# A layer norm's row chain and its scaling step cut into two column halves, in a macaron transformer layer on 8 cores

## The chip, the cores and the metric

The kernel runs on all 8 cores of one Trainium2 chip. The metric is the device time in microseconds of the slowest core, for one execution. A profile adds, for each core, the span from its first to its last instruction and the mean clock that was granted to TensorE.

## What is computed

One macaron layer over 2 x 4096 rows of width 2048: half a feed-forward block, an attention block, half a feed-forward block, each behind a layer norm.

```python
def _layernorm(x, axis=-1, eps=1e-5):
    m = jnp.mean(x, axis=axis, keepdims=True)
    v = jnp.var(x, axis=axis, keepdims=True)
    return (x - m) / jnp.sqrt(v + eps)
...
def _L0_ffn_ref(x, U, V, W1, b1, W2, b2):
    h = jax.nn.relu(jnp.einsum('bsd,de->bse', x, W1) + b1)
    alpha = jax.nn.softmax(jnp.einsum('bse,ek->bsk', h, W2) + b2, axis=-1)
    vx = jnp.einsum('krd,bsd->bskr', V, x)
    uvx = jnp.einsum('kdr,bskr->bskd', U, vx)
    return jnp.einsum('bsk,bskd->bsd', alpha, uvx)
...
x = x + 0.5 * _L0_ffn_ref(_layernorm(x), ...)
x = x + _L0_attn_ref(_layernorm(x), ...)
x = x + 0.5 * _L0_ffn_ref(_layernorm(x), ...)
```

The attention has 16 heads over a latent of 64 columns, is causal, and adds half of the logits again within a band of 64 rows.

## The kernel before

Activations lie transposed: the 2048 features are 16 chunks (`NCH`) of 128 partitions, and 1024 rows of the batch (`NTOK`) are the columns, so a chunk is 128 x 1024. Cores 0 to 3 share one batch element and cores 4 to 7 the other; each core owns 1024 of its 4096 rows. Since attention needs keys and values of all 4096 rows, every core computes the first feed-forward block, the second layer norm and the key/value projection for all four quarters. That is a loop over j = 0 to 3; the last quarter is the core's own, and stays in `x_res` (f32). Then come the query projection, the attention over 16 heads, the output projection, and the second feed-forward block with the third layer norm. So a core runs nine layer norms: two for each j, and one at the end.

Every engine runs its own program in the order in which the code writes it. Each `@block.<engine>` appends to one engine. Order between engines is made by semaphores alone: `ct` counts TensorE (PE in the profile), `cs` ScalarE (ACT), `cv` VectorE (DVE), `dx`, `dw0` and `dw1` the transfers. There is no scheduler.

One layer norm is `emit_ln`:

- For each chunk, ScalarE squares it (L176), and TensorE sums the chunk over the partitions with a column of ones, in f32 (L183, L186), and the squares in bf16 (L190, L192). This leaves two rows of 1 x 1024 in PSUM, `ln_sum` and `ln_sq`.
- The row chain follows. VectorE makes the mean (L199), its square (L202), takes EPS off (L205), and subtracts from the mean of the squares (L208). ScalarE takes Ln (L215) and Exp with scale -0.5 (L217), which gives 1/sqrt(var + eps). Each step works on all 1024 columns and waits for the step before it.
- VectorE makes `mrr`, the row of -mean/std (L224), which later matmuls add as a correction. TensorE spreads the row of 1/std over 128 partitions with two f32 matmuls of 512 columns (L230, L232), into `ln_rrep`.
- VectorE multiplies each of the 16 chunks with `ln_rrep` into the bf16 `xhat` (L242). These 16 instructions are called the applies below. The mean isn't subtracted here; the correction through `mrr` does that.
- At its end `emit_ln` calls `load_fence` (L136), which makes TensorE and ScalarE wait until the last apply is done:

```python
load_fence(block, ('tensor', 'scalar'), cv.h, last)
return last, apply_toks, mr_tok
```

What follows a layer norm is one of three. In `emit_big_proj` (L318), 16 output tiles are made from 16 chunks in two halves of 512 columns, with a semaphore wait ahead of each chunk of the first tile (`rhs_ready`). For the first j and for the last layer norm, 16 matmuls that sum the weights' columns (`bp_cs`, L288) stand ahead of it. After the second layer norm of each j, the key/value projection comes first (L778), with its own wait for each chunk. Weights come over the GpSimd queue (L274), whose first two loads of a projection wait for TensorE's count at the entry, which is the second L232. SP loads the next quarter of x (L753); each of the four loads waits for the apply that read its chunks last.

Of the kernel before, what the change touches and what calls it, by code (L numbers as in the profile page):

```python
# [8 lines left out]
F32 = mybir.dt.float32  # L9
# [3 lines left out]
AF = mybir.ActivationFunctionType  # L13
ALU = mybir.AluOpType
# [136 lines left out]
def emit_ln(nc, block, bufs, S, src_chunks, dst, wait0=None, mrr=None):  # L151
# [5 lines left out]
    with contextlib.ExitStack() as ps:  # L157
# [7 lines left out]
        rstd = ps.enter_context(nc.sbuf_tensor(f"ln_r{u}", [1, NTOK], F32))  # L165
        sq_toks = []
# [29 lines left out]
        @block.vector  # L196
        def _(v):
# [3 lines left out]
            v.wait_ge(cv.h, cv.n + 1)  # L201
            v.tensor_tensor(t2[:, :], m_sb[:, :], m_sb[:, :],  # L202
                            ALU.mult).then_inc(cv.h, 1)
            v.wait_ge(cv.h, cv.n + 2)
            v.tensor_scalar(t2[:, :], t2[:, :], EPS, None,  # L205
                            ALU.subtract).then_inc(cv.h, 1)
            v.wait_ge(cv.h, cv.n + 3)
            v.scalar_tensor_tensor(t2[:, :], p_sq[:, :], 1.0 / E, t2[:, :],  # L208
                                   ALU.mult, ALU.subtract).then_inc(cv.h, 1)
        cv.inc(3)  # L210
        var_tok = cv.inc()
        @block.scalar
        def _(s):
            s.wait_ge(cv.h, var_tok)
            s.activation(rstd[:, :], t2[:, :], AF.Ln).then_inc(cs.h, 1)  # L215
            s.wait_ge(cs.h, cs.n + 1)
            s.activation(t2[:, :], rstd[:, :], AF.Exp,  # L217
                         scale=-0.5).then_inc(cs.h, 1)
        cs.inc(1)
        rstd_tok = cs.inc()  # L220
# [6 lines left out]
        @block.tensor  # L227
        def _(t):
            t.wait_ge(cs.h, rstd_tok)
            t.matmul(p_rrep[:, 0:512], bufs['onesr_f'][:, :], t2[:, 0:512],  # L230
                     start=True, stop=True)
            t.matmul(p_rrep[:, 512:1024], bufs['onesr_f'][:, :],  # L232
                     t2[:, 512:1024], start=True, stop=True).then_inc(ct.h, 1)
        rep_tok = ct.inc()
        last = None
        apply_toks = []
        for c in range(NCH):
            @block.vector
            def _(v, c=c):
                if c == 0:  # L240
                    v.wait_ge(ct.h, rep_tok)
                v.tensor_mul(dst[:, NTOK * c:NTOK * (c + 1)], src_chunks[c],  # L242
                             p_rrep[:, :]).then_inc(cv.h, 1)
            last = cv.inc()
            apply_toks.append(last)
        load_fence(block, ('tensor', 'scalar'), cv.h, last)
        return last, apply_toks, mr_tok


def emit_big_proj(nc, block, bufs, S, wq_dram, rhs_sb, out_cb,  # L250
# [7 lines left out]
    with contextlib.ExitStack() as ps:  # L258
# [21 lines left out]
        for q in range(4):  # L280
# [18 lines left out]
            for mc in range(4):  # L299
# [3 lines left out]
                def _(t, q=q, mc=mc, m=m, par=par):  # L303
# [286 lines left out]
def alloc_common(nc, e):  # L590
# [11 lines left out]
    b['consts'] = e(nc.sbuf_tensor("consts_sb", [1, 2], F32))  # L602
# [34 lines left out]
def build_fused():  # L637
# [20 lines left out]
    di('consts', [1, 2])  # L658
# [10 lines left out]
    with contextlib.ExitStack() as stx:  # L669
# [20 lines left out]
        with contextlib.ExitStack() as ph1:  # L690
# [50 lines left out]
            for j in range(4):  # L741
                xq_toks = []
                for qd in range(4):
# [15 lines left out]
                _, ln1_ap, mr1 = emit_ln(nc, block, bufs, S, x_chunks, xhat,  # L759
                                         wait0=w0, mrr=mrr1)  # L760
                res_toks = emit_ffn(nc, block, bufs, S, x_chunks, xhat,
                                    dr['varr'], dr['uarr'],
                                    rhs_ready=[(cv.h, t) for t in ln1_ap],
# [812 lines left out]
def _prep_weights(Wq, Wk, Wv, q2l, vup, Wo, U, V, W1, b1, W2, b2):  # L1576
# [22 lines left out]
    w['consts'] = np.array([[-0.5, 0.0]], np.float32)  # L1599
    return w  # L1600


# [40 lines left out]
```

## Time and profile before

| | us |
|---|---|
| median of 3 runs | 3466.84 |
| lowest, highest | 3461.24, 3523.13 |
| the profiled execution, its own time | 3458.73 |
| its span, slowest core (core 5) | 3457.2 |
| spans of the 8 cores | 3431.9 to 3457.2 |
| TensorE busy (core 5) | 2826.2, 82% |
| VectorE busy | 1118.8, 32% |
| ScalarE busy | 699.4, 20% |

The profile shows one execution. Busy time counts instructions, overlapping ones once; "idle before" a group names what ended the wait of its engine. The granted clock of TensorE is 1.00 for 2.4 GHz and 0.50 for 1.2 GHz; a value between is a mean over a stretch.

### The profile page before, as it was taken

The page shows a single profiled execution, that of the slowest core. Times are in us where ns is not written, and L with a number is a line of the kernel's source. Part 1 is how long each engine was busy: PE and PEld are TensorE (multiplying, and loading weights), DVE is VectorE, ACT ScalarE, POOL GpSimd, SP SyncE. Part 2 cuts the span into 40 slices and gives each one's busy share as a digit, 9 for nine tenths or more (in the row PEclk, how much of TensorE's full clock was granted, in tenths as well). Part 3 has the DMA queues.
Part 4 walks back from the last instruction along what each step waited for, and adds up shares of the span by engine and source line. Part 5 has one row for each costly group of instructions (what it writes and reads, how often), then busy time and mean ns, then how long its engine had stood idle before and what let it go on. Part 6 is the DMA issues. An engine that isn't in the chain of part 4 may idle for free.

```text
span 3457.2 us, 31819 instructions; the slowest of 8 cores (3431.9 to 3457.2 us)
## 1 busy us (share of the span) xinstructions
PE 2826.2 (82%) x10719; PEld 1003.3 (29%) x10719; DVE 1118.8 (32%) x2081; ACT 699.4 (20%) x1149; POOL 51.3 (1%) x78
## 2 busy tenths in 40 slices
PE   4988679866986698597488888888888888697986
PEld 1433123312331243132122222222222222242332
DVE  2003320322032203212345455554555444312003
ACT  2111211021102110200133333333333333302110
POOL 0000000000000000000000000000000000000000
PEclk8999889988988898798555555555655555698998
DMA  5320244024402331140000000000000000131322
GB/s 139 64 49 0 100 73 73 0 101 73 73 1 101 64 62 21 21 80 14 17 1 1 1 1 1 1 1 1 1 1 1 1 1 1 31 67 24 75 49 98
DMA packets 14786, 128.16 MB, mean 37 GB/s; under 512 B 6369, under 2 KB 6682, under 8 KB 7562
## 3 DMA queue, kind: packets, MB, share of 16 engines
q0 software_dynamic: 6848, 82.28, 13.0%
q1 hardware_dynamic: 7786, 43.83, 3.5%
q8 instruction: 97, 1.59, 0.2%
q14 instruction: 55, 0.45, 0.0%
HBM read 196.53 MB, written 9.27 MB: 60 GB/s over the span
## 4 chain that ended last, share of the span: by engine, by line
PE 77%; DVE 12%; DMA 3%; issue 3%; ACT 3%; DVEq 0%; POOL 0%; ACTq 0%; SPq 0%; POOLq 0%
PE bp_p L318 23%; PE PD L1469 7%; PE PB L1466 7%; PE PC L1390 6%; DVE xhat L242 5%; PE fe_p L573 4%; PE fe_p L515 4%; PE ln_sum L183 4%; PE ln_sum L186 4%; PE PC L1425 3%; PE PA L1255 2%; PE PA L1304 1%; PE bp_p L331 1%; PE bp_cs L288 1%; PE kv_ps L778 1%
## 5 line engine op out<-in xcount | busy, mean ns | idle before, releaser
L318 PE MATMUL bp_p<-xhat,wslotP 128*128 128x512 bf16 x2560 | 574.5, 383 | 56.3 <-DVE xhat L242 56.3
L1447 ACT ACTIVATE probs<-PC 128x512 bf16<-128x512 f32 (+3 forms) x768 | 353.4, 488 | 816.2 <-PE PC L1425 460.4
L318 PEld LDWEIGHTS bp_p<-xhat,wslotP 128*128 128x128 bf16 x2560 | 245.9, 99 | 383.1 <-issue 104.5
L1469 PE MATMUL PD<-probs,vexp 128*128 128x512 bf16 (+3 forms) x768 | 356.0, 464 | 0.0
L1466 PE MATMUL PB<-probs,ones_bf 128*1 128x512 bf16 (+3 forms) x768 | 342.4, 446 | 12.5 <-ACT probs L1447 12.3
L1390 PE MATMUL PC<-qlat_h,kaug 65*128 65x256 bf16 (+3 forms) x1088 | 325.0, 397 | 24.9 <-ACT probs L1447 24.2
L176 ACT ACTIVATE ln_sq<-x_res 128x1024 bf16<-128x1024 f32 x144 | 152.2, 1057 | 720.3 <-DVE x_res L583 317.8
L1425 PE MATMUL PC<-mr,ident_bf 128*128 128x256 bf16 (+1 forms) x576 | 185.9, 345 | 82.5 <-DVE mr L1408 80.2
L1408 DVE COPY_PREDICATED mr<-bandm_sb,ob 128x256 bf16<-128x256 uint8 (+1 forms) x512 | 210.7, 412 | 113.0 <-DVE ob L1348 63.8
L358 ACT ACTIVATE bbuf<-bp_p,b_sb 128x1024 bf16<-128x1024 f32 x80 | 89.3, 1116 | 673.1 <-PE bp_p L331 673.1
L1390 PEld LDWEIGHTS PC<-qlat_h,kaug 65*128 65x128 bf16 x1088 | 126.2, 122 | 166.8 <-issue 154.6
L242 DVE TENSOR_TENSOR xhat<-x_res,ln_rrep 128x1024 bf16<-128x1024 f32 x144 | 163.7, 1215 | 24.2 <-PE ln_rrep L232 24.2
L183 PE MATMUL ln_sum<-x_res,ones_f 128*1 128x512 f32 x288 | 147.9, 595 | 16.2 <-DMA x_res<-xall 8.3
L186 PE MATMUL ln_sum<-x_res,ones_f 128*1 128x512 f32 x288 | 147.9, 595 | 0.0
L412 DVE TENSOR_SCALAR ffn_zsb<-kv_ps,b_sb 8x1024 f32<-8x1024 f32 x4 | 5.1, 1272 | 440.0 <-PE kv_ps L402 440.0
L1469 PEld LDWEIGHTS PD<-probs,vexp 128*128 128x128 bf16 x768 | 78.0, 102 | 228.6 <-issue 213.5
L1348 DVE TENSOR_SCALAR ob<-qshrepb,ksumT 128x256 bf16<-128x256 bf16 (+1 forms) x512 | 139.8, 273 | 0.0
L1425 PEld LDWEIGHTS PC<-mr,ident_bf 128*128 128x128 bf16 x576 | 69.8, 123 | 207.5 <-issue 197.4
L318 PE MATMUL bp_p<-bbuf,wslotF 128*128 128x512 bf16 x512 | 112.8, 384 | 18.4 <-DMA wslotF<-woq 18.4
L573 PE MATMUL fe_p<-ffn_vx,wslotP 128*128 128x512 bf16 x512 | 119.6, 399 | 6.6 <-DVE ffn_vx L555 6.6
L1466 PEld LDWEIGHTS PB<-probs,ones_bf 128*1 128x1 bf16 x768 | 60.7, 79 | 207.5 <-issue 190.3
L515 PE MATMUL fe_p<-xhat,wslotP 128*128 128x512 bf16 x512 | 118.4, 391 | 0.9 <-DVE vsum L498 0.9
(167 smaller groups left out, 2099.1 us busy)
## 6 DMA issues: line engine op xcount, KB each, us to landing
x_res<-xall SPq DMA_DIRECT2D x16, 2048.0 KB, 7.9
wslotP<-w1q POOLq DMA_DIRECT2D x16, 2048.0 KB, 13.9
wslotP<-varr POOLq DMA_DIRECT2D x4, 2048.0 KB, 14.2
wslotP<-uarr POOLq DMA_DIRECT2D x4, 2048.0 KB, 13.7
wslotP<-wqq POOLq DMA_DIRECT2D x4, 2048.0 KB, 13.2
wslotF<-woq POOLq DMA_DIRECT2D x4, 2048.0 KB, 14.7
wslotF<-w1q POOLq DMA_DIRECT2D x4, 2048.0 KB, 14.8
wslotF<-varr POOLq DMA_DIRECT2D x1, 2048.0 KB, 13.3
```

The source lines that it names most:

```text
L183: t.matmul(p_sum[:, 0:512], bufs['ones_f'][:, 0:1], src_chunks[c][:, 0:512], start=(c == 0), stop=(c == NCH - 1))
L186: t.matmul(p_sum[:, 512:1024], bufs['ones_f'][:, 0:1], src_chunks[c][:, 512:1024], start=(c == 0), stop=(c == NCH - 1))
L242: v.tensor_mul(dst[:, NTOK * c:NTOK * (c + 1)], src_chunks[c], p_rrep[:, :]).then_inc(cv.h, 1)
L318: mi = t.matmul(P[par][:, 512 * half:512 * half + 512], lhsT, rhs_sb[:, NTOK * k + 512 * half: NTOK * k + 512 * half + 512], start=(k == 0 ...
L515: mi = t.matmul(P[par][:, 512 * half:512 * half + 512], lhsT, xhat[:, NTOK * k + 512 * half: NTOK * k + 512 * half + 512], start=(k == 0), ...
L573: mi = t.matmul(P[par][:, 512 * half:512 * half + 512], lhsT, vx[:, NTOK * j + 512 * half: NTOK * j + 512 * half + 512], start=(j == 0), s ...
L1390: mi = t.matmul(PC[:, a + dlt:b + dlt], kaug[0:65, 128 * i:128 * i + 128], ql[0:65, a:b], start=first, stop=stop)
L1408: v.copy_predicated(mr_sb[r][:, 0:lead], bandm_sb[:, 256 * r:256 * r + lead], ob_sb[i % 2][:, 0:lead]).then_inc(cv.h, 1)
L1425: mi = t.matmul(PC[:, a + dlt:b + dlt], bufs['ident_bf'][:, :], mr_sb[i % 4][:, a - qlo:b - qlo], start=False, stop=True)
L1447: s.activation(probs[i % 2][:, a:b], PC[:, a + dlt:b + dlt], AF.Exp).then_inc(cs.h, 1)
L1466: t.matmul(PB[:, a:b], bufs['ones_bf'][:, 0:1], probs[i % 2][:, a:b], start=(i == 0), stop=last)
L1469: mi = t.matmul(PD[:, a:b], vex[:, 128 * i:128 * i + 128], probs[i % 2][:, a:b], start=(i == 0), stop=last)
```

## The change

The row chain is cut into columns 0 to 511 and 512 to 1023. VectorE makes mean, square and variance of the first half, then of the second; the instruction that took EPS off is gone, and EPS comes in as the bias of Ln, from a third element of the small constant tensor. ScalarE does Ln and Exp for each half. TensorE's two spreading matmuls wait each for its half. `mrr` stays one instruction of 1024 columns. Each apply becomes two of 512 columns, the second right behind the first. In the first tile of `emit_big_proj`, a dictionary of tokens lets each half of a chunk have its own wait; where a list is given, the wait moves from ahead of the first half to ahead of the second. The `load_fence` at the end of `emit_ln` stands as before.

```diff
-            v.wait_ge(ct.h, mm_toks[-1])
-            v.tensor_scalar(m_sb[:, :], p_sum[:, :], 1.0 / E,
-                            None, ALU.mult).then_inc(cv.h, 1)
...
-            v.tensor_scalar(t2[:, :], t2[:, :], EPS, None,
-                            ALU.subtract).then_inc(cv.h, 1)
...
+        for (lo, hi) in halves:
+            @block.vector
+            def _(v, lo=lo, hi=hi):
+                if lo == 0:
+                    v.wait_ge(ct.h, mm_toks[-1])
+                v.tensor_scalar(m_sb[:, lo:hi], p_sum[:, lo:hi], 1.0 / E,
+                                None, ALU.mult).then_inc(cv.h, 1)
+                v.wait_ge(cv.h, cv.n + 1)
+                v.tensor_tensor(t2[:, lo:hi], m_sb[:, lo:hi], m_sb[:, lo:hi],
+                                ALU.mult).then_inc(cv.h, 1)
+                v.wait_ge(cv.h, cv.n + 2)
+                v.scalar_tensor_tensor(t2[:, lo:hi], p_sq[:, lo:hi], 1.0 / E,
+                                       t2[:, lo:hi], ALU.mult,
+                                       ALU.subtract).then_inc(cv.h, 1)
...
+                s.activation(rstd[:, lo:hi], t2[:, lo:hi], AF.Ln,
+                             bias=bufs['consts'][0:1, 2:3]).then_inc(cs.h, 1)
+                s.wait_ge(cs.h, cs.n + 1)
+                s.activation(t2[:, lo:hi], rstd[:, lo:hi], AF.Exp,
+                             scale=-0.5).then_inc(cs.h, 1)
...
+                t.wait_ge(cs.h, rh)
+                t.matmul(p_rrep[:, lo:hi], bufs['onesr_f'][:, :],
+                         t2[:, lo:hi], start=True,
+                         stop=True).then_inc(ct.h, 1)
...
         for c in range(NCH):
...
+            for hf, (lo, hi) in enumerate(halves):
+                @block.vector
+                def _(v, c=c, hf=hf, lo=lo, hi=hi):
+                    if c == 0:
+                        v.wait_ge(ct.h, rep_h[hf])
+                    v.tensor_mul(dst[:, NTOK * c + lo:NTOK * c + hi],
+                                 src_chunks[c][:, lo:hi],
+                                 p_rrep[:, lo:hi]).then_inc(cv.h, 1)
+                last = cv.inc()
+                apply_hk[(c, hf)] = last
             apply_toks.append(last)
         load_fence(block, ('tensor', 'scalar'), cv.h, last)
-        return last, apply_toks, mr_tok
+        return last, apply_toks, mr_tok, apply_hk
...
-                        if m == 0 and rhs_ready is not None:
-                            t.wait_ge(rhs_ready[k][0], rhs_ready[k][1])
                         lhsT = wv[:, k, 128 * mc:128 * mc + 128]
                         for half in range(2):
+                            if m == 0 and rhs_ready is not None:
+                                rr = rhs_ready[(k, half)] \
+                                    if isinstance(rhs_ready, dict) \
+                                    else (rhs_ready[k] if half == 1
+                                          else None)
+                                if rr is not None:
+                                    t.wait_ge(rr[0], rr[1])
```

VectorE's order in the first layer norm, before. `ln_m` is the mean, `ln_t` the row that becomes 1/std; the last row is the first of 16 applies.

```order
L199 TENSOR_SCALAR ln_m<-ln_sum 1x1024 [waits ct]
L202 TENSOR_TENSOR ln_t<-ln_m 1x1024 [waits cv]
L205 TENSOR_SCALAR ln_t<-ln_t 1x1024 [waits cv]
L208 SCALAR_TENSOR_TENSOR ln_t<-ln_sq,ln_t 1x1024 [waits cv]
L221 UNCONDITIONAL_BRANCH
L224 SCALAR_TENSOR_TENSOR mrr<-ln_m,ln_t 1x1024 [waits cs]
L238 UNCONDITIONAL_BRANCH
L242 TENSOR_TENSOR xhat<-x_res,ln_rrep 128x1024 [waits ct]
```

The same place after.

```order
L203 TENSOR_SCALAR ln_m<-ln_sum 1x512 [waits ct]
L206 TENSOR_TENSOR ln_t<-ln_m 1x512 [waits cv]
L209 SCALAR_TENSOR_TENSOR ln_t<-ln_sq,ln_t 1x512 [waits cv]
L199 UNCONDITIONAL_BRANCH
L203 TENSOR_SCALAR ln_m<-ln_sum 1x512
L206 TENSOR_TENSOR ln_t<-ln_m 1x512 [waits cv]
L209 SCALAR_TENSOR_TENSOR ln_t<-ln_sq,ln_t 1x512 [waits cv]
L225 UNCONDITIONAL_BRANCH
L228 SCALAR_TENSOR_TENSOR mrr<-ln_m,ln_t 1x1024 [waits cs]
L245 UNCONDITIONAL_BRANCH
L249 TENSOR_TENSOR xhat<-x_res,ln_rrep 128x512 [waits ct]
```

Four rows of 1024 columns have become six of 512, and `mrr` still stands ahead of every apply and waits for the Exp of the second half.

TensorE's order from the spreading matmuls to the first tile behind the first layer norm, before.

```order
L230 MATMUL ln_rrep<-ln_t,onesr_f 128x512 [waits cs]
L232 MATMUL ln_rrep<-ln_t,onesr_f 128x512
L136 UNCONDITIONAL_BRANCH
L283 UNCONDITIONAL_BRANCH [waits cv]
L288 MATMUL bp_cs<-wslotP,ones_bf 1x512 [waits dw0]
```

The same place after.

```order
L236 MATMUL ln_rrep<-ln_t,onesr_f 128x512 [waits cs]
L233 UNCONDITIONAL_BRANCH
L236 MATMUL ln_rrep<-ln_t,onesr_f 128x512 [waits cs]
L136 UNCONDITIONAL_BRANCH
L292 UNCONDITIONAL_BRANCH [waits cv]
L297 MATMUL bp_cs<-wslotP,ones_bf 1x512 [waits dw0]
L311 UNCONDITIONAL_BRANCH
L332 MATMUL bp_p<-xhat,wslotP 128x512 [waits dw0,cv]
L332 MATMUL bp_p<-xhat,wslotP 128x512 [waits cv] x31
```

The second spreading matmul now has a wait of its own; the wait for `cv` that comes from the fence stands at the same place in both, ahead of everything that reads `xhat`.

## Rows read from the trace of the kernel before

**Rows 1.** Spans of some cores: span, mean granted TensorE clock
```profile
core 5: 3457.2 us, clock 0.762
core 6: 3431.9 us, clock 0.770
```

**Rows 2.** Who waited for the applies (L242), core 5: us in total, times
```profile
  PE kv_ps L778: 75.2, 4
...
  PE bp_p L318: 56.3, 3
  PE bp_cs L288: 37.1, 2
```

**Rows 3.** Timeline of the first layer norm: start us, us, engine, line [idle before <-releaser]
```profile
57.35 1.21 DVE L199 TENSOR_SCALAR ln_m<-ln_sum 1x1024 f32<-1x1024 f32 x1 [44.34 <-PE ln_sq L192]
58.67 1.21 DVE L202 TENSOR_TENSOR ln_t<-ln_m 1x1024 f32<-1x1024 f32 x1
59.99 0.68 DVE L205 TENSOR_SCALAR ln_t<-ln_t 1x1024 f32<-1x1024 f32 x1
60.78 1.21 DVE L208 SCALAR_TENSOR_TENSOR ln_t<-ln_sq,ln_t 1x1024 f32<-1x1024 f32 x1
62.09 1.06 ACT L215 ACTIVATE ln_r<-ln_t 1x1024 f32<-1x1024 f32 x1 [5.83 <-DVE ln_t L208]
63.23 1.06 ACT L217 ACTIVATE ln_t<-ln_r 1x1024 f32<-1x1024 f32 x1
64.39 1.21 DVE L224 SCALAR_TENSOR_TENSOR mrr<-ln_m,ln_t 1x1024 bf16<-1x1024 f32 x1 [2.40 <-ACT ln_t L217]
...
64.43 2.04 PE L230 MATMUL ln_rrep<-ln_t,onesr_f 1*128 1x512 f32 x2 [7.19 <-ACT ln_t L217]
...
66.27 1.91 PE L232 MATMUL ln_rrep<-ln_t,onesr_f 1*128 1x512 f32 x2
...
68.29 18.19 DVE L242 TENSOR_TENSOR xhat<-x_res,ln_rrep 128x1024 bf16<-128x1024 f32 x16 [2.68 <-PE ln_rrep L232]
...
86.73 4.91 PE L288 MATMUL bp_cs<-wslotP,ones_bf 128*1 128x512 bf16 x16 [18.55 <-DVE xhat L242]
```

**Rows 4.** Groups by line and shape: xcount, busy us, mean ns of one
```profile
L242 DVE TENSOR_TENSOR xhat<-x_res,ln_rrep 128x1024 bf16<-128x1024 f32 x144 | 163.7, 1215 | 24.2 <-PE ln_rrep L232 24.2
L1286 ACT ACTIVATE rcp_row<-sums_sb 1x512 f32<-1x512 f32 x32 | 20.2, 630 | 47.3 <-DVE sums_sb L1280 46.1 <-DVE ob L1348 1.2
L1113 ACT ACTIVATE cb_sb<-cfin,hlk 1x1024 f32<-1x1024 f32 x16 | 18.4, 1150 | 1.5
```

**Rows 5.** Timeline of VectorE at three places with 512 columns back to back
```profile
1641.04 0.68 DVE L914 CAST ksum_bf<-ks_ps 1x512 bf16<-1x512 f32 x1 [1.26 <-PE kn_ps L907]
1641.64 0.67 DVE L920 TENSOR_REDUCE kmt<-kn_ps 1x1 f32<-1x512 f32 x1
1642.42 0.15 DVE L926 TENSOR_TENSOR km<-km,kmt 1x1 f32<-1x1 f32 x1
...
1766.95 0.68 DVE L1321 TENSOR_TENSOR bbuf<-rep_sb,PD 128x512 bf16<-128x512 f32 x1
1767.55 0.28 DVE L1348 TENSOR_SCALAR ob<-qshrepb,ksumT 128x256 bf16<-128x256 bf16 x1
```

**Rows 6.** The chain that ended last: a pair of f32 matmuls at full clock
```profile
55.10 0.86 PE ln_sum L183 x2
```

**Rows 7.** Stretches in the chain, core 5: busy times, then granted clock, DMA share, GB/s
```profile
62.00:63.00 1.00, 0.00 (x0) 0.00 (x0) 0.00 (x0) 0.91 (x1) 0.00 (x0) 0.54 0.00 0
3175.00:3177.00 2.00, 0.00 (x0) 0.00 (x0) 1.79 (x3) 0.00 (x0) 0.00 (x0) 0.51 0.00 0
```

**Rows 8.** Timeline of TensorE: the first tile behind a layer norm, and the next
```profile
91.57 7.08 PE L318 MATMUL bp_p<-xhat,wslotP 128*128 128x512 bf16 x32
...
99.12 7.08 PE L318 MATMUL bp_p<-xhat,wslotP 128*128 128x512 bf16 x32
...
385.68 9.07 PE L778 MATMUL kv_ps<-xhat,wkv_sb 128*128 128x512 bf16 x32 [18.76 <-DVE xhat L242]
...
459.44 9.73 PE L318 MATMUL bp_p<-xhat,wslotP 128*128 128x512 bf16 x32 [18.76 <-DVE xhat L242]
```

**Rows 9.** DMA issues: KB each, median us to landing
```profile
wslotP<-w1q POOLq DMA_DIRECT2D x16, 2048.0 KB, 13.9
```

**Rows 10.** The attention stage on cores 5 and 6, columns as in rows 7
```profile
1620.00:3010.00 1390.00, 1164.68 (x4067) 377.17 (x4067) 684.04 (x1646) 428.71 (x866) 20.55 (x21) 0.57 0.01 2
1620.00:3010.00 1390.00, 1133.79 (x4037) 380.20 (x4102) 684.46 (x1647) 424.59 (x865) 17.65 (x20) 0.58 0.02 5
```

More of the change, by code:

```diff
@@ L165, in emit_ln @@
         rstd = ps.enter_context(nc.sbuf_tensor(f"ln_r{u}", [1, NTOK], F32))
+        halves = ((0, 512), (512, 1024))
         sq_toks = []
@@ L210, in emit_ln, with _ @@
[L210 to L220, printed above, removed]
+        rstd_h = []
+        for (lo, hi) in halves:
[12 more added lines that the diff above has]
+                                       ALU.subtract).then_inc(cv.h, 1)
+            cv.inc(2)
+            var_tok = cv.inc()
+            @block.scalar
+            def _(s, lo=lo, hi=hi, var_tok=var_tok):
+                s.wait_ge(cv.h, var_tok)
+                s.activation(rstd[:, lo:hi], t2[:, lo:hi], AF.Ln,
[3 more added lines that the diff above has]
+                             scale=-0.5).then_inc(cs.h, 1)
+            cs.inc(1)
+            rstd_h.append(cs.inc())
@@ L221, in _ @@
+        rstd_tok = rstd_h[1]
         @block.vector
@@ L226, in emit_ln, with _ @@
         mr_tok = cv.inc()
[L227 to L234, printed above, removed]
+        rep_h = []
+        for hf, (lo, hi) in enumerate(halves):
+            @block.tensor
+            def _(t, lo=lo, hi=hi, rh=rstd_h[hf]):
+                t.wait_ge(cs.h, rh)
+                t.matmul(p_rrep[:, lo:hi], bufs['onesr_f'][:, :],
+                         t2[:, lo:hi], start=True,
+                         stop=True).then_inc(ct.h, 1)
+            rep_h.append(ct.inc())
         last = None
         apply_toks = []
+        apply_hk = {}
         for c in range(NCH):
[L238 to L244, printed above, removed]
+            for hf, (lo, hi) in enumerate(halves):
+                @block.vector
[7 more added lines that the diff above has]
+                apply_hk[(c, hf)] = last
             apply_toks.append(last)
         load_fence(block, ('tensor', 'scalar'), cv.h, last)
-        return last, apply_toks, mr_tok
+        return last, apply_toks, mr_tok, apply_hk
 def emit_big_proj(nc, block, bufs, S, wq_dram, rhs_sb, out_cb,
@@ L758, in build_fused @@
                 w0 = [(dx.h, xq_toks[c // 4]) for c in range(NCH)]
-                _, ln1_ap, mr1 = emit_ln(nc, block, bufs, S, x_chunks, xhat,
-                                         wait0=w0, mrr=mrr1)
+                _, ln1_ap, mr1, ln1_hk = emit_ln(
+                    nc, block, bufs, S, x_chunks, xhat, wait0=w0, mrr=mrr1)
                 res_toks = emit_ffn(nc, block, bufs, S, x_chunks, xhat,
                                     dr['varr'], dr['uarr'],
-                                    rhs_ready=[(cv.h, t) for t in ln1_ap],
+                                    rhs_ready={k: (cv.h, t)
+                                               for k, t in ln1_hk.items()},
                                     mrr=mrr1, mr_tok=mr1,
@@ L766, in build_fused @@
                 w2l = [(cv.h, res_toks[c]) for c in range(NCH)]
-                _, ln2_q, mr2 = emit_ln(nc, block, bufs, S, x_chunks, xhat,
-                                        wait0=w2l, mrr=mrr2)
+                _, ln2_q, mr2, _h2 = emit_ln(
+                    nc, block, bufs, S, x_chunks, xhat, wait0=w2l, mrr=mrr2)
                 if True:
@@ L1550, in build_fused @@
                 nc.psum_tensor("zps2", [128, NTOK], F32))
-            _, ln3_ap, mr3 = emit_ln(nc, block, bufs, S, x_chunks, xhat3,
-                                     wait0=(cv.h, wo_last), mrr=mrr3)
+            _, ln3_ap, mr3, ln3_hk = emit_ln(
+                nc, block, bufs, S, x_chunks, xhat3,
+                wait0=(cv.h, wo_last), mrr=mrr3)
             ffn2_res = emit_ffn(nc, block, bufs, S, x_chunks, xhat3,
                                 dr['varr'], dr['uarr'],
-                                rhs_ready=[(cv.h, t) for t in ln3_ap],
+                                rhs_ready={k: (cv.h, t)
+                                           for k, t in ln3_hk.items()},
                                 mrr=mrr3, mr_tok=mr3, first=True, zps=zps2)
@@ L1598, in _prep_weights @@
     w['onesr'] = np.ones((1, 128), np.float32)
-    w['consts'] = np.array([[-0.5, 0.0]], np.float32)
+    w['consts'] = np.array([[-0.5, 0.0, EPS]], np.float32)
     return w
```

13 lines of the change are left out of this document (2 added, 11 removed).

## The prediction

> **What bounds the kernel now.** I read the spans of the cores first [rows 1]: eight cores run the same program and end 25 us apart, with clocks from 0.762 to 0.770, so no single core is held up by something of its own. TensorE is busy 82% of the span, VectorE 32%. On average TensorE is the bound, but an average says nothing of the stage that is changed. So I next asked who waited for the applies [rows 2]: TensorE, in all nine layer norms, 75.2 + 56.3 + 37.1 = 168.6 us, or 18.7 us each. That is as long as the 16 applies themselves. Hence in these stretches VectorE sets the pace, and what is saved or added there counts in full.
>
> The timeline of one layer norm gives the path [rows 3]. The last `ln_sq` matmul releases L199 at 57.35. The row chain runs to 68.29, where the first apply starts; the applies take 18.19 us and end at 86.48; TensorE goes on at 86.73. From L199 to the end of the last apply it is 29.13 us. The other eight layer norms have the same pieces: the nine idle times of L242 sum to 24.2 us, 2.69 each [rows 4], as in rows 3. The sum below therefore compares one layer norm, before and after, and takes the difference nine times. Times in it count from the start of the first mean instruction.
>
> **The row chain, step by step.** A dependent step on VectorE starts 0.10 to 0.11 us after the end of the one before (57.35 + 1.21 to 58.67), ScalarE starts 0.10 behind VectorE, its second function 0.08 behind its first, and VectorE 0.10 behind ScalarE [rows 3]. A 512-column row instruction with one result per cycle takes 0.68, and where the next one doesn't depend on it, the next starts 0.60 after its start (1641.04 to 1641.64, from PSUM, across a branch between two blocks as here) [rows 5].
>
> First half on VectorE: 0.79 + 0.79 + 0.68 = 2.26. Second half: its mean doesn't wait, so it starts 0.60 after the third instruction's start, at 1.58 + 0.60 = 2.18, and the three end at 2.18 + 2.26 = 4.44. The EPS step (0.68 and a hop of 0.11) is gone.
>
> ScalarE: a 512-column function takes 0.63; with a bias read from memory, 1024 columns took 1.15 where 1.06 stands without [rows 3, 4], so I give the Ln 0.72. (Without that extra the chain is 0.09 shorter for each layer norm, below 1 us in all.) First half: Ln from 2.36 to 3.08, Exp from 3.16 to 3.79. Second half: Ln waits for 4.44, so it runs from 4.54 to 5.26, and Exp from 5.34 to 5.97. The first half's work on ScalarE is hidden beside VectorE's second half.
>
> TensorE: the first spreading matmul starts at 3.93 (0.14 behind ScalarE, as 63.23 + 1.06 to 64.43) and takes 1.84 to 2.04 at the low clock, so it is done by 5.97; the second starts at 6.11 and ends 1.91 later, at 8.02 [rows 3]. VectorE makes `mrr` from 6.07, the next instruction can start 1.13 later, at 7.20. The first half apply (chunk 0, half 0) thus runs at 7.20, hidden before the second matmul's end, and the second half apply starts at 8.13.
>
> **The applies.** Sixteen took 18.19 us at 1.215 each: successive starts are (18.19 - 1.215)/15 = 1.132 apart [rows 3, 4], which is 1024 columns at 1.067 us and 0.065 more. No trace of before shows a long row of 512-column applies. The nearest row is L1321, a TENSOR_TENSOR of 128x512 with one operand in PSUM like an apply: 0.68 long, and the next instruction, in a block of its own, starts 0.60 behind its start [rows 5]. The lower bound is 0.57, half of 1.13 with nothing added (8 us more gained in all); the upper bound is 0.79, a start that waits for the end and a hop, as at 1641.64 to 1642.42. I take 0.60, since two pairs of rows agree on it. Behind the half apply at 8.13 thirty more follow: the last starts at 8.13 + 30 x 0.60 = 26.1 and ends at 26.8.
>
> So one layer norm ends at 26.8 instead of 29.1: 2.35 us earlier. In parts, the first full chunk's worth starts 10.94 - 8.13 = 2.8 us earlier, one half apply is done by then (0.6), and thirty-two fixed parts instead of sixteen cost about 1.0 of it back. Nine times 2.35 is 21 us.
>
> The spreading matmuls can be faster than this. At the granted clock of 1.00 a pair of such f32 instructions takes 0.86 [rows 6], not 1.84. Before, they ran at 0.50, since they came 7.2 us after the last matmul, and the clock had fallen by then: to 0.54 at 62 to 63 us in the first layer norm, but to 0.51 at 3175 to 3177 in the last [rows 7], that is some 2 to 5 us after the last matmul. Now the first one comes 4 us after it. Where the clock still stands, the second matmul ends at 7.1, and the applies run on from `mrr` without a gap: second half at 7.80, 0.33 less. With all nine it is 3 us more; with about a third of them, 1 us. I take 22 us for the whole.
>
> The Trainium skill speaks against the splitting, in "VectorE: DVE Perf Modes", section "The DRAIN you can't avoid": the next VectorE operation doesn't start until the pipe behind the one before is empty; its section "The TRN2 errata — SBUF-src ops pay a fixed extra latency per instruction" adds that many small tiles pay the fixed part for each. Rows 5 show the next operation starting at 0.60 of 0.68, before the end, so the trace bears out a smaller fixed part than the first rule has; the second rule's direction agrees. The first rule's result is the first rival below.
>
> **What the rest costs.** The extra waits ahead of every matmul of the first tile: with one wait for two matmuls, the 32 took 7.08 us, and the next tile without waits took 7.08 [rows 8]; both waits are long fulfilled behind the fence. I cost them at nothing; if each of 16 extra waits showed as one 0.03 hop, 0.5 us in each of five projections would be 2.5 us more. They stand on TensorE alone, and nothing else is queued behind them but the tile. The moved wait in the query projection is fulfilled too. The weights of the first tile are issued after the second spreading matmul and land 13.9 later [rows 9]: at 8.0 + 0.5 + 13.9 = 22.4, still ahead of the last apply at 26.8. Nothing new is late there. SP's loads of x follow the applies' tokens and are ahead by the same 2 us; behind them lie 9 us of key/value matmuls. The first tile or projection behind a layer norm runs partly at the low clock (9.73 and 9.07 against 7.08) [rows 8]; TensorE is still idle for some 18 us there, so this stays.
>
> **Against the runs.** The sum is made against the profiled execution: 3458.7 - 22 = 3436.7. That execution lies 8 us under the median of three and 2.5 under the lowest; the undisturbed values are 3458.7, 3461.2 and 3466.8, mean 3462.3. I give 3462.3 - 22 = 3440.
>
> **The rivals.**
>
> Halves that cost as much as their length. If a half apply holds the next one until its end (0.685), the last apply ends at 8.13 + 30 x 0.685 + 0.68 = 29.4, 0.2 later than before, and nothing is left: 3464. If each also pays a hop (0.79), it ends at 32.5, 3.4 later, nine times 30 us: 3492, slower than before. The point from which it decides is (29.13 - 8.13 - 0.68)/30 = 0.677. For it: independent pairs of 512 columns are few in the trace, and each apply stands in its own block with a branch. Against it: both pairs in rows 5 have that branch and start at 0.60.
>
> The finer gating works. If TensorE could start at the first half chunk, its first work would lie beside the applies and end about 0.4 us behind the last. That saves some 9.3 us for three layer norms (9.73 less 0.4), 8.7 for the four before key/value (9.07 less 0.4), and 4.91 + 7.08 - 0.4 = 11.6 for the two with column sums [rows 3, 8]: 86 us, and 3354. Against it: the wait behind L136 stands at the same place in both orders, and the key/value projection, which has a wait for each chunk already, still idles until the last apply [rows 2]. That the change doesn't do what its tokens say is what I expect.
>
> The gain is lost in the attention stage. This stage holds the low clock most of the time, and the same program differs there by 1164.7 to 1133.8 us of busy TensorE between two cores [rows 10]. If shorter rests for TensorE earlier, or another phase of the clock, cost 1% of this stage on the slowest core, 12 us go back, and with the spread of single runs it looks like no change: 3452 to 3462. For it: 25 us between cores. Against it: all cores gain alike, and the slowest of eight varied by only 8 us between undisturbed runs.
>
> **How the numbers follow.** Forecast (halves at about 0.60, 15 to 30 us gained): 0.73. Gain lost in the attention stage: 0.13. Halves at their full length, no gain: 0.06; with a hop, slower by 30 us: 0.04. Gating works: 0.02. Something else: 0.02. The range of 8 in 10 goes from 3424 (30 us gained, with the lower bound of the applies, and a run 8 us below the mean) to 3464 (the case of no gain). A change under 2% can't well be told from none here, 2% being 69 us: only the gating case passes it on the fast side, so faster 0.02, and nothing that I can price passes it on the slow side, so slower 0.01, and 0.97 is left for within 2%.
>
> **What would show it.** In the profile of the changed kernel: 32 applies in about 19.3 us of which the last 31 start 0.60 apart; from the first mean to the last apply's end 26.8 us; TensorE idle behind it still with L249 as the one that ends it, about 18 us or a little more; the second Exp ending 6.0 after the first mean; the first tile at the same 7.08 or 9.7. The forecast is wrong if the applies start more than 0.68 apart, if TensorE's wait for them is short, or if the time in the attention stage moves by more than the layer norms gain.

## The result

| | before | changed |
|---|---|---|
| median of 26 runs each, us | 3472.0 | 3449.3 |
| lowest | 3459.9 | 3439.6 |
| ratio, with its 95% interval | | 0.9937 (0.9915 to 0.9959) |

0.63% less, some 22 us. Executions in which the cores of a die get a lower clock than the others are left out of the ratio; the first profile of the changed kernel was such a one, so the rows below are from its second, run e1 (own time 3442.6).

The timeline of the first layer norm after the change, core 1, answers to [rows 3].

```profile
58.28 0.68 DVE L203 TENSOR_SCALAR ln_m<-ln_sum 1x512 f32<-1x512 f32 x1 [45.49 <-PE ln_sq L193]
...
60.46 0.67 DVE L203 TENSOR_SCALAR ln_m<-ln_sum 1x512 f32<-1x512 f32 x1
60.63 0.72 ACT L217 ACTIVATE ln_r<-ln_t,consts_sb 1x512 f32<-1x512 f32 x1 [3.45 <-DVE ln_t L209]
...
62.21 4.21 PE L236 MATMUL ln_rrep<-ln_t,onesr_f 1*128 1x512 f32 x4 [4.04 <-ACT ln_t L220]
62.79 0.72 ACT L217 ACTIVATE ln_r<-ln_t,consts_sb 1x512 f32<-1x512 f32 x1 [0.72 <-DVE ln_t L209]
63.60 0.63 ACT L220 ACTIVATE ln_t<-ln_r 1x512 f32<-1x512 f32 x1
64.33 1.21 DVE L228 SCALAR_TENSOR_TENSOR mrr<-ln_m,ln_t 1x1024 bf16<-1x1024 f32 x1 [1.64 <-ACT ln_t L220]
65.48 0.67 DVE L249 TENSOR_TENSOR xhat<-x_res,ln_rrep 128x512 bf16<-128x512 f32 x1
66.53 18.62 DVE L249 TENSOR_TENSOR xhat<-x_res,ln_rrep 128x512 bf16<-128x512 f32 x31 [0.38 <-PE ln_rrep L236]
...
85.40 6.55 PE L297 MATMUL bp_cs<-wslotP,ones_bf 128*1 128x512 bf16 x16 [18.98 <-DVE xhat L249]
```

The second half's mean starts 2.18 behind the first's; the second Exp ends at 64.23, 5.95 behind; the long row of applies starts at 8.25 and ends at 85.15. From first mean to last apply it is 26.87 us, where it was 29.13. The other layer norms agree: over all nine and all eight cores it is 26.85 to 26.87 in e1, and was 29.11 to 29.13.

Who ended TensorE's idle time after the change, core 1, answers to [rows 2]: us in total, times, longest.

```profile
PE kv_ps L793 <- DVE xhat L249: 76.8, 4, 19.2
PE bp_p L332 <- DVE xhat L249: 57.6, 3, 19.2
PE bp_cs L297 <- DVE xhat L249: 38.0, 2, 19.0
```

TensorE waits 172.4 us for the applies, 19.2 for each layer norm, a little longer than before: the finer waits don't let it start earlier.

To see where the rest of the time moved, I cut each core's span at the first mean instruction (L199 or L203) of the first, eighth and ninth layer norm and took the mean over the eight cores, in us. The last column is the mean of the spans in the profiled execution.

| kernel | first to eighth | eighth to ninth (attention in it) | ninth to end | mean span |
|---|---|---|---|---|
| before | 1359.7 | 1743.7 | 284.0 | 3445.9 |
| e1, changed | 1339.9 | 1745.7 | 280.6 | 3425.2 |
| e2, chain only | 1338.2 | 1744.8 | 280.7 | 3422.9 |
| e3, applies only | 1362.7 | 1748.3 | 285.8 | 3455.4 |
| e4, no fence | 1304.7 | 1737.1 | 277.0 | 3377.7 |
| e7, early weights, fence | 1339.2 | 1754.3 | 283.6 | 3436.0 |

The middle stretch, in which the attention lies, differs by 20 to 34 us between the cores of one of these executions (before: 1734.5 to 1754.9; e1: 1731.7 to 1762.3), so its means by some us too. The first stretch differs by 6 us between the cores of before, and by less than 2 between those of e1. The difference between before and e1 lies in the outer two.

### The profile page after: what moved, and what is told of

The parts are those of the page before. It is cut to its first block, busy times and chain, and to the rows that moved or that the text cites. A ratio compares the mean times of both kernels' runs of the same rounds, so it can differ in the third digit from the quotient of the medians.

```text
span 3579.9 us, 32124 instructions; the slowest of 8 cores (3514.5 to 3579.9 us)
## 1 busy us (share of the span) xinstructions
PE 2967.8 (83%) x10719; PEld 1029.5 (29%) x10719; DVE 1124.9 (31%) x2243; ACT 703.3 (20%) x1167; POOL 51.2 (1%) x78
## 4 chain that ended last, share of the span: by engine, by line
PE 79%; DVE 11%; DMA 3%; issue 3%; ACT 3%; DVEq 0%; POOL 0%; ACTq 0%; SPq 0%; POOLq 0%
PE bp_p L332 24%; PE PD L1484 7%; PE PB L1481 7%; PE PC L1405 6%; DVE xhat L249 5%; PE fe_p L529 4%; PE fe_p L587 4%; PE ln_sum L184 4%; PE ln_sum L187 4%; PE PC L1440 3%; PE PA L1270 2%; PE bp_p L345 2%; PE PA L1319 1%; PE bp_cs L297 1%; PE kv_ps L793 1%
## 5 line engine op out<-in xcount | busy, mean ns | idle before, releaser
L332 PE MATMUL bp_p<-xhat,wslotP 128*128 128x512 bf16 x2560 | 644.1, 416 | 57.6 <-DVE xhat L249 57.6
L332 PEld LDWEIGHTS bp_p<-xhat,wslotP 128*128 128x128 bf16 x2560 | 261.2, 104 | 438.2 <-issue 325.6
L1405 PE MATMUL PC<-qlat_h,kaug 65*128 65x256 bf16 (+3 forms) x1088 | 328.2, 401 | 26.3 <-ACT probs L1462 25.9
L249 DVE TENSOR_TENSOR xhat<-x_res,ln_rrep 128x512 bf16<-128x512 f32 x288 | 173.6, 680 | 3.4 <-PE ln_rrep L236 3.4
L184 PE MATMUL ln_sum<-x_res,ones_f 128*1 128x512 f32 x288 | 159.1, 636 | 18.0 <-DMA x_res<-xall 10.1
L187 PE MATMUL ln_sum<-x_res,ones_f 128*1 128x512 f32 x288 | 158.3, 633 | 0.0
L587 PE MATMUL fe_p<-ffn_vx,wslotP 128*128 128x512 bf16 x512 | 129.7, 423 | 6.6 <-DVE ffn_vx L569 6.6
L529 PE MATMUL fe_p<-xhat,wslotP 128*128 128x512 bf16 x512 | 132.9, 426 | 0.9 <-DVE vsum L512 0.9
```

Source lines behind the costliest of these rows:

```text
L184: t.matmul(p_sum[:, 0:512], bufs['ones_f'][:, 0:1], src_chunks[c][:, 0:512], start=(c == 0), stop=(c == NCH - 1))
L187: t.matmul(p_sum[:, 512:1024], bufs['ones_f'][:, 0:1], src_chunks[c][:, 512:1024], start=(c == 0), stop=(c == NCH - 1))
L249: v.tensor_mul(dst[:, NTOK * c + lo:NTOK * c + hi], src_chunks[c][:, lo:hi], p_rrep[:, lo:hi]).then_inc(cv.h, 1)
L332: mi = t.matmul(P[par][:, 512 * half:512 * half + 512], lhsT, rhs_sb[:, NTOK * k + 512 * half: NTOK * k + 512 * half + 512], start=(k == 0 ...
L529: mi = t.matmul(P[par][:, 512 * half:512 * half + 512], lhsT, xhat[:, NTOK * k + 512 * half: NTOK * k + 512 * half + 512], start=(k == 0), ...
L587: mi = t.matmul(P[par][:, 512 * half:512 * half + 512], lhsT, vx[:, NTOK * j + 512 * half: NTOK * j + 512 * half + 512], start=(j == 0), s ...
```

## The experiments

Twelve runs were made, of nine kernels: e1 is the changed kernel, and e10, e11 and e12 repeat e5, e6 and e8. "Mean span" is the mean over the eight cores in the profiled execution.

**e1, the changed kernel again.**

> The changed kernel once more, for an undisturbed profile beside its parts. My account (2.35 us less for each of nine layer norms): 20 to 25 us under before; from the first mean instruction to the end of the last apply 26.8 us where the spreading matmuls run at the low clock, 26.4 where they run at full clock; applies 0.60 apart; PE's wait for the applies 18 to 19.5 us in every layer norm. The rival, that the gain comes from finer gating of the first tile, wants that wait to be shorter than the applies are long. The rival that the attention stage gives or takes something wants a difference outside the layer norms of more than 5 us on the same core.

Measured: ratio 0.9931 (0.9895 to 0.9966), mean span 20.7 us less. 26.87 us for a layer norm, the wait 19.2. Nine times 2.26 is 20.3, close to the 20.7, but that closeness is in part luck. The two outer stretches hold eight layer norms, which gives 18.1, and they gained 23.2; the middle one holds the ninth's 2.3 and is 2.0 longer instead, well inside its own scatter. Where the outer ones got more is taken up behind e3. The rival by finer gating falls: the wait grew.

**e2, the row chain alone in halves.** The applies are those of before, and wait for the second spreading matmul.

```diff
-            for hf, (lo, hi) in enumerate(halves):
...
+            @block.vector
+            def _(v, c=c):
+                if c == 0:
+                    v.wait_ge(ct.h, rep_h[1])
+                v.tensor_mul(dst[:, NTOK * c:NTOK * (c + 1)], src_chunks[c],
+                             p_rrep[:, :]).then_inc(cv.h, 1)
```

> The row chain in halves, but the 16 applies at 1024 columns each, as before, the first one waiting for the second spreading matmul. My account: the applies start 8.13 us after the first mean (10.94 before) and take 18.2 again, so the end is at 26.3: 2.8 us less than before for each layer norm, 25 us in all (up to 30 where the spreading matmuls are at full clock), and 4 us faster than the full change. If instead the split of the applies is what brings the gain, this kernel is slower than the full change by 10 us or more.

Ratio 0.9922 (0.9861 to 0.9983), mean span 23.0 less than before. The times can't part it from e1; the timeline of core 7 can:

```profile
60.10 0.68 DVE L203 TENSOR_SCALAR ln_m<-ln_sum 1x512 f32<-1x512 f32 x1 [46.29 <-PE ln_sq L193]
...
68.35 18.18 DVE L248 TENSOR_TENSOR xhat<-x_res,ln_rrep 128x1024 bf16<-128x1024 f32 x16 [0.98 <-PE ln_rrep L236]
```

Applies start at 8.25 and end at 26.43, 0.44 earlier than with half applies. The chain brings the whole gain. (In the seventh layer norm all cores start the spreading matmuls and the applies 0.36 later; I don't know why.)

**e3, the applies alone in halves.**

```diff
+            for lo, hi in ((0, 512), (512, 1024)):
...
+                    v.tensor_mul(dst[:, NTOK * c + lo:NTOK * c + hi],
+                                 src_chunks[c][:, lo:hi],
+                                 p_rrep[:, lo:hi]).then_inc(cv.h, 1)
```

> Only the applies are cut in two; the chain, the EPS step and the waits of the first tile stay as before. My account: 31 starts 0.60 apart and 0.68 at the end make 19.3 instead of 18.19, so 1.1 us more for each layer norm, 10 us slower than before. If halves cost nothing, the time is that of before; if each held the next until its end (0.685), 3.7 us more for each, 33 us slower.

Ratio 1.0002 (0.9962 to 1.0042), mean span 9.5 more than before. By its time alone this is no verdict; the timeline of core 3 gives the size. The last row is its second layer norm.

```profile
58.59 1.21 DVE L199 TENSOR_SCALAR ln_m<-ln_sum 1x1024 f32<-1x1024 f32 x1 [45.56 <-PE ln_sq L192]
...
69.53 19.22 DVE L243 TENSOR_TENSOR xhat<-x_res,ln_rrep 128x512 bf16<-128x512 f32 x32 [2.68 <-PE ln_rrep L232]
...
385.74 8.50 PE L780 MATMUL kv_ps<-xhat,wkv_sb 128*128 128x512 bf16 x32 [19.79 <-DVE xhat L243]
```

Successive starts are (19.22 - 0.68)/31 = 0.598 apart, against 1.132 for full width. By itself the split costs VectorE 1.03 us for each layer norm, 9.3 us for nine; in the changed kernel, where the first half apply is hidden ahead of the second spreading matmul, it is the 0.44 of e2.

That the mean span is 9.5 longer, near these 9.3, is luck: 4.6 of it lie in the middle stretch, and the first is 3.0 longer, not 7 x 1.03 = 7.2. The missing part was given back by TensorE. The key/value burst in the last row above takes 8.50, where the same one took 9.07 in the kernel before [rows 8]. So I added up, for the first seven layer norms, how long behind its first mean instruction each one's applies end, and the work right behind them (the key/value burst or the first tile, up to the first matmul that reads `mrr`). Means over eight cores, us less than before:

| kernel | applies end | work behind them ends | first stretch |
|---|---|---|---|
| e1, changed | 15.8 | 17.7 | 19.8 |
| e2, chain only | 18.5 | 21.1 | 21.5 |
| e3, applies only | -7.2 | -3.4 | -3.0 |

The second column accounts for the stretches of e2 and e3 within 0.4; of the 4.0 that e1 has beyond its applies, it explains 1.9.

**e4, without the fence.** The full change, and

```diff
-        load_fence(block, ('tensor', 'scalar'), cv.h, last)
         return last, apply_toks, mr_tok, apply_hk
```

with `cs_ps` allocated ahead of `P` in `emit_big_proj`.

> The full change, and the wait at the end of the layer norm, which holds TensorE and ScalarE until the last apply, is gone; what reads xhat has its own waits for each chunk. (The one-bank PSUM tile of the column sums is allocated ahead of the output tiles, so that nothing overlaps the spread row while it is read.) My account, by which this fence makes the finer waits idle: the first tile or the key/value projection lies beside the applies, and the column sums too; 9.3 us less for three layer norms, 8.7 for four, 11.6 for two, 86 in all, so about 108 under before. If TensorE's low clock stays longer, because it now works thinly during the applies, up to 2.7 us each of this is lost, and it is 80 under before. If the fence isn't what holds TensorE (the per-chunk waits were, or the weights' arrival), the time is that of the changed kernel.

Ratio 0.9875 (0.9735 to 1.0014), unclear by its times; its mean span is 47.5 us under e1, little more than half of the expected 86. Core 3 shows why. After the second layer norm of a quarter, TensorE takes chunk after chunk beside the applies:

```profile
361.79 18.62 DVE L249 TENSOR_TENSOR xhat<-x_res,ln_rrep 128x512 bf16<-128x512 f32 x31 [0.38 <-PE ln_rrep L236]
362.62 1.01 PE L792 MATMUL kv_ps<-xhat,wkv_sb 128*128 128x512 bf16 x2 [0.94 <-DVE xhat L249]
...
381.08 0.60 PE L799 MATMUL kv_ps<-mrr,wkvsum 1*128 1x512 bf16 x2
```

Ahead of the feed-forward projection it doesn't:

```profile
60.51 0.68 DVE L203 TENSOR_SCALAR ln_m<-ln_sum 1x512 f32<-1x512 f32 x1 [46.73 <-PE ln_sq L193]
...
86.46 5.48 PE L296 MATMUL bp_cs<-wslotP,ones_bf 128*1 128x512 bf16 x16 [17.81 <-DMA wslotP<-w1q]
```

The weights let TensorE go on at 25.95 behind the first mean, 0.9 us ahead of the last apply. Core 3 is a late one; the same place on core 1:

```profile
79.81 5.28 PE L296 MATMUL bp_cs<-wslotP,ones_bf 128*1 128x512 bf16 x16 [13.97 <-DMA wslotP<-w1q]
```

Over the eight cores and the first, third, fifth and seventh layer norm, the first weights land 20.9 to 26.3 behind the first mean, 23.2 on the mean; the applies end at 26.86. The fence held TensorE, as I had it; behind it stood a second limit, 0.6 to 6 us shorter.

**e5, no fence and early weights.** e4, and the first two loads of the projection wait for the sums of the 12th chunk.

```diff
+        bufs['load_after'] = mm_toks[11]
...
-        entry_ct = ct.n
+        entry_ct = ct.n if load_after is None else load_after
```

> The changed kernel without the fence at the end of the layer norm, and with the first two weight loads of the feed-forward projection released by the 12th chunk's sums instead of by the spreading matmuls, some 17 us earlier. The run without the fence alone gained for the key/value projection, but the first tile of the projection then waited for its weights until just before the last apply. If that is all that held it, three tiles end 7 us earlier and the two with column sums 11 us, so 43 us under that run: a mean span of 3335 us over the cores, a time near 3355, and some 110 us under before. If TensorE's clock stays low behind a tile that is fed thinly, 2.6 us of each of five is lost: 30 us under that run. If the weights were not the limit, no difference to it.

Ratio 0.9710 (0.9642 to 0.9778). The weights now land 4.2 to 9.7 us behind the first mean and hold TensorE for at most 1.7 us. But the mean span, 3356.6, is only 21 us under e4, less even than the lower expectation. That expectation took core 3's late arrival of the weights for all cores; over nine layer norms the work behind the applies ends 31 us earlier than in e4, not 43. And the five second tiles take 45.0 us together, where they took 5 x 7.08 = 35.4: there TensorE's clock is low. See e6 and e9.

**e6, the same with full applies.**

> As the last one, but the applies at 1024 columns. If finer waits bring something once the fence is gone, the half applies should win: the tile ends one matmul instead of two behind the last apply (0.4 us at the low clock). The applies themselves end 0.4 us earlier at full width. So by my account the two are the same within 2 us over nine layer norms, and the finer waits are worth nothing beyond the waits for each chunk. If the half waits matter, this one is slower by 5 us or more.

Ratio 0.9653 (0.9596 to 0.9710).

**e7, early weights with the fence.**

> The changed kernel with the fence, with the weight loads earlier. With the fence the weights land before the last apply, so my account says no difference to the changed kernel, within 3 us. If weights landing behind the applies cost something in the changed kernel, this is faster by the idle time that is saved; if the earlier loads delay the loads of x in the first layer norm, up to 5 us slower.

Ratio 0.9940 (0.9893 to 0.9987), as e1. The stretch from the first to the eighth layer norm is 1339.2 against 1339.9: no difference, as expected. Its mean span is 10.8 us above e1: 8.6 of it in the attention's stretch, which this edit doesn't touch, and 3.0 behind the ninth layer norm. I read the first as scatter; the 3.0 stay unexplained.

**e8, the kernel before with the fence gone and early weights.**

> The kernel before (chain and applies at 1024 columns, EPS step) without the fence and with the weight loads earlier. My account: the same gain as e6 from the overlap, but the row chain 2.8 us longer in each of nine layer norms, 25 us slower than e6. If the gain of the row chain is hidden once TensorE works beside the applies, the two are the same.

Ratio 0.9751 (0.9681 to 0.9820).

**e9, pairs.** e5, with `ln1_hk[(k[0], 1)]` as the token for both halves.

> e5 (no fence, early weights, half applies) with one change: the first tile's matmuls wait for both halves of a chunk, so they come in pairs, 1.20 us apart. In e5, where single matmuls come 0.60 apart, the second tile ran partly at the low clock (8.68 us), in e6 (full applies, pairs 1.13 apart) not (7.08). If single matmuls are what keeps TensorE's clock low, this kernel's second tile takes 7.08 in most layer norms. If the pace is, the clock in the applies' stretch stays as in e5, 0.50 to 0.85, and the second tile is slow in most. The key/value projection, in pairs in both, already speaks for the pace.

Ratio 0.9746 (0.9672 to 0.9821).

**e10, e11, e12: e5, e6 and e8 once more**, on one chip with e9.

> e5 once more, for the comparison of its time with e6 on one chip: the half applies with finer waits. By the clocks of the first profiles (0.90 over the first 1500 us against 0.92 and 0.93) it is slower than e6, by 10 to 20 us. If the first difference was chance, the two are within 5 us.

> e6 once more: full applies, the row chain in halves, no fence, early weights. If TensorE's clock stays up beside full applies, it is the fastest of all, near 3358 undisturbed, 0.965 to 0.97 of before.

> e8 once more: the old row chain with the fence gone and early weights. It should be 25 us slower than e6 if the row chain's 2.8 us still count in each of nine layer norms; if they are hidden, the same.

| | first ratio | again |
|---|---|---|
| e5, e10: half applies | 0.9710 (0.9642 to 0.9778) | 0.9717 (0.9662 to 0.9772) |
| e6, e11: full applies | 0.9653 (0.9596 to 0.9710) | 0.9711 (0.9656 to 0.9765) |
| e8, e12: old chain, full applies | 0.9751 (0.9681 to 0.9820) | 0.9765 (0.9693 to 0.9836) |

The intervals overlap, so the times rank these three only weakly: e6 before e5 by 0.6% and then by 0.1%, and before e8 by 1.0% and 0.5%. For the row chain the segments say more: from the first to the eighth layer norm e11 took 1273.7 and e12 1295.1, 21.4 us for seven layer norms, near the 7 x 2.7 = 18.9 of the chain. So in this stretch the chain counts without the fence too, and e8 has the same 1294.9. (In the profile of e6 itself cores 6 and 7 took 1325.7 and 1323.5 and the other six 1270.8 to 1278.2; its mean is 1286.0.) The middle stretch went the other way in these profiles, 1747.1 in e11 against 1737.8 in e12 and 1728.6 in e8, so their mean spans (3349.2, 3366.7 and 3355.8) don't show the 21 us in full.

For half against full applies the clock says more. The same layer norm (the first of the second quarter), core 5, in e10 with half applies:

```profile
414.30 10.85 DVE L250 TENSOR_TENSOR xhat<-x_res,ln_rrep 128x512 bf16<-128x512 f32 x18 [0.38 <-PE ln_rrep L237]
...
415.13 18.52 PE L332 MATMUL bp_p<-xhat,wslotP 128*128 128x512 bf16 x31 [0.40 <-DVE xhat L250]
433.58 1.03 PE L345 MATMUL bp_p<-mrr,msum_w 1*128 1x512 bf16 x2
434.55 8.96 PE L332 MATMUL bp_p<-xhat,wslotP 128*128 128x512 bf16 x32
```

In e11 with full applies:

```profile
411.20 6.41 PE L330 MATMUL bp_p<-xhat,wslotP 128*128 128x512 bf16 x12 [1.47 <-DVE xhat L249]
417.99 0.59 PE L330 MATMUL bp_p<-xhat,wslotP 128*128 128x512 bf16 x2 [0.38 <-DVE xhat L249]
...
429.23 7.08 PE L330 MATMUL bp_p<-xhat,wslotP 128*128 128x512 bf16 x32
```

And the same stretch in e9, half applies with paired matmuls:

```profile
414.60 1.01 PE L332 MATMUL bp_p<-xhat,wslotP 128*128 128x512 bf16 x2 [0.94 <-DVE xhat L250]
...
427.75 0.59 PE L332 MATMUL bp_p<-xhat,wslotP 128*128 128x512 bf16 x2 [0.18 <-DVE xhat L250]
...
433.60 7.08 PE L332 MATMUL bp_p<-xhat,wslotP 128*128 128x512 bf16 x32
```

Granted clock over these applies and then over the second tile (stretch, length, busy time of PE, PEld, DVE, ACT, POOL, clock, DMA share, GB/s), in the order e10, e11, e9:

```profile
413.25:432.90 19.65, 18.86 (x33) 3.22 (x31) 19.27 (x33) 0.00 (x0) 0.00 (x0) 0.50 0.44 67
433.60:443.40 9.80, 9.80 (x35) 3.62 (x34) 0.00 (x0) 1.11 (x1) 0.00 (x0) 0.76 0.01 2
```

```profile
409.80:428.20 18.40, 11.17 (x31) 3.03 (x31) 18.19 (x16) 0.00 (x0) 0.00 (x0) 0.80 0.51 76
428.70:436.70 8.00, 8.00 (x37) 3.26 (x36) 0.00 (x0) 1.11 (x1) 0.00 (x0) 1.00 0.01 2
```

```profile
412.70:432.40 19.70, 14.45 (x32) 3.05 (x30) 19.31 (x33) 0.00 (x0) 0.00 (x0) 0.62 0.53 80
433.10:441.10 8.00, 8.00 (x37) 3.23 (x36) 0.00 (x0) 1.12 (x1) 0.00 (x0) 1.00 0.01 2
```

With half applies the clock stayed at 0.50 beside all the applies, and the second tile took 8.96; with full applies it rose to 1.00 some 8 us in and stayed, and the tile took 7.08. Core 5 of e10 lost some 40 us later in this quarter, but the stretch shown is not special: cores 0 and 7, which didn't, also have 0.50 there, and 8.97 and 8.93 for the second tile. On all eight cores of e11 the applies' stretches show 0.78 to 0.92, in e10 0.50 to 0.87. Of the 40 second tiles (five for each core), 38 took 7.08 in e11, and none did in e10 (8.67 to 10.19).

Pairs alone, in e9, change part of it. 22 of the 40 second tiles took 7.08: all 16 behind the third and seventh layer norm, none behind the fifth. But the applies' stretches show 0.50 to 0.91: the clock rose late here (0.62), and on the same core it stayed at 0.50 in four later stretches. So of the two accounts that were set against each other, the tiles speak for the one by single matmuls and the clock beside the applies for the one by the pace. In time nothing is gained: 0.9746, and a mean span of 3358.9 against 3356.6 in e5 and 3374.8 in e10.

The key/value matmuls come in pairs in all these kernels. With half applies they are 1.20 us apart: in e10 the clock was 0.50 over the whole stretch in 19 of 32, and in the fourth layer norm of e5 it stayed there for twelve of sixteen pairs (cores 0, 5 and 7). With full applies, 1.13 apart, it rose after three or four pairs, and e11 shows 0.85 to 0.87 in all 32. So the pace of the feed goes with the clock. It doesn't decide it alone, since three of the 32 in e10 show 0.87 at the same 1.20; and that it is the cause, rather than the moment at which the stretch begins, I have not shown separately.

## Why the prediction was right

**Who bounds the stretch.** Right. VectorE did before and does after: TensorE waits for the applies in all nine layer norms of before, e1, e2 and e3, and the applies end 2.7 us earlier with the chain alone and 1.03 later with the split alone.

**The row chain.** Right: second Exp at 5.95 (5.97), applies at 8.25 (8.13). The Ln with a bias took 0.72, as the row of another activation said. Missing from my chain is 0.12 us ahead of the second apply: the second spreading matmul now starts behind a rest and takes 2.04, as the first does, where I gave it the 1.91 of one that follows another.

**The applies.** Right: 0.598 apart (0.60). The full-length rival needed 0.68, and the slower one 0.79. The Trainium skill's rule ("VectorE: DVE Perf Modes", section "The DRAIN you can't avoid"), that the next operation waits until the pipe is empty, is not what these independent applies show: 0.68 long, 0.598 apart. The same section says that an operation that isn't held starts earlier, which agrees with them and which my prediction left out. The Trainium skill's section on the fixed latency per instruction ("The TRN2 errata — SBUF-src ops pay a fixed extra latency per instruction", the same page) has the direction right, and e3 gives the size, (19.22 - 18.19)/16 = 0.064 us for each added instruction.

**The spreading matmuls at full clock.** Wrong in its place, and small. In the third layer norm of e1 the first one did run at full clock on five of the eight cores, here core 1:

```profile
428.20 1.09 PE L236 MATMUL ln_rrep<-ln_t,onesr_f 1*128 1x512 f32 x2 [4.04 <-ACT ln_t L220]
...
430.36 2.04 PE L236 MATMUL ln_rrep<-ln_t,onesr_f 1*128 1x512 f32 x2 [1.07 <-ACT ln_t L220]
```

But the second, on which the applies hang, was at the low clock in all nine: VectorE's idle time ahead of the long row of applies is 3.4 us in nine times, 0.38 each. So the 1 us that I added for it was not there. What came instead lies behind the applies, where the clock rises sooner. On core 5, which shows most of it, the four key/value bursts take 34.6 us in e1 against 36.4 before, and the three first tiles 26.8 against 29.3 [rows 8 have one of each]; on cores 1, 2, 3, 4 and 7 it is 35.2 to 36.1 and 27.1 to 27.5 (the traces of cores 0 and 6 lack some of these matmuls). On the mean that is half of the 4 us by which the first stretch gains more (19.8) than seven times 2.26 (15.8), as the table behind e3 has it; the other half I can't place. I had left the time behind the applies as it was. The row chain isn't what raised the clock sooner: e3, whose chain is that of before and whose TensorE rests longer (19.8 us against 18.8), shows it more strongly, with 34.6 to 34.7 and 26.7 to 26.9 on all of these cores. What does is open.

**The finer gating.** The mechanism was right: the fence makes the finer waits idle. The price of a gate that works, 86 us, was right only for TensorE's first work, and only with early weights: in e5 the work behind the applies ends 85.9 us earlier than in e1 over nine layer norms. Removing the fence alone gave 54.8 in this measure and 47.5 in the mean span. The step that failed is in the sum of that rival: it puts the first tile and the column sums beside the applies from the start, although by the arrival that I had worked out myself, 22.4, the weights leave them only the last 4.4 us. They arrived at 20.9 to 26.3, so 22.4 was 0.8 short on the mean. In e4 the three first tiles ended 3.9 us earlier each where I had 9.3, the two with column sums 4.7 where I had 11.6, and the key/value bursts, whose weights are not loaded there, 8.4 where I had 8.7. The second term that failed was put at nothing: the clock behind the applies. It made the five second tiles 9.6 us longer in e5, and the mean span gained 68.6, not 85.9; with full applies (e11) it gained 76.0.

**The attention stage.** Its scatter is real, 20 to 34 us between cores of one execution, and the mean over cores moved by 2.0 against the gain. That is within the scatter, so a loss of a few us there is neither shown nor excluded.

**The forecast.** 22 us less was measured as 0.9937, which is 21.8 on the 3462.3 from which I started; the interval, 0.9915 to 0.9959, allows 14 to 29. So close a hit is in part luck: 1 us of the 22 was for spreading matmuls that stayed at the low clock, and the time that TensorE saved behind the applies was not in the sum. The median of 26 runs lies 9 us above my 3440, because my starting value, a mean of three executions, lay 10 us under the later median of before (3472.0 against 3462.3).

## What to carry to other kernels

Before making waits finer, look for a coarser one that stands ahead of them in the engine's order: here the gain came only from the halved serial chain, while cutting the 16 wide instructions delayed the last apply by 0.44 us in each layer norm (1.03 by itself) and gained nothing. When a wait is removed, ask what would have ended it next, and put that into the price: here the weights' arrival had been worked out and was left out of the sum. Look at it on all cores, since it differed by 5 us between them. And when a sum hits the total, compare its parts too: e1 and e3 agreed with the sum in total better than in their stretches. Of the variants run, the one without the fence, with early weights, the halved chain and full-width applies is faster than both kernels: 0.9653 and 0.9711 of before, with both intervals below 0.98, where the changed kernel has 0.9937.

## What was not expected of the hardware

Work fed to TensorE in thin slices beside VectorE left its clock at 0.50 for a whole stretch of 19 us (e10); nearly the same work fed 6% faster, in pairs, brought it to 1.00 within some 8 us (e11). Of the 72 stretches of applies (nine on each of eight cores), 33 of e10 show 0.50 throughout, and none of e11. Pairs at the slower pace (e9) lie between. So a finer split of the feeding engine's work may cost time on TensorE too; whether it does so by its pace, by single matmuls or by when it begins is open.
